# The product of maximum and scale in the softmax: from VectorE, behind the maximum, to ScalarE, ahead of the exponentials

## The chip, the cores and the metric

The kernel runs on one core of a Trainium2 chip. The metric is the device time of one execution in microseconds. Three runs of the kernel before took 1253.99, 1259.27 and 1259.77 us, median 1259.27 us.

## The reference

Two layers work on x, 2 batches of 2048 tokens of width 512 in float32. With ctx a context of 128 tokens per batch, and each branch scaled by the tanh of a gate:

```python
x = x + tanh(g_xattn[0]) * L0_xattn(layernorm(x), ctx)     # rotary cross attention, 8 heads of 64, softmax over 128
x = x + tanh(g_ffn[0])   * L0_ffn(layernorm(x))            # ternary weights, low-rank part, relu squared, 512 -> 2048 -> 512
x = x + tanh(g_xattn[1]) * L1_xattn(layernorm(x), ctx)     # linear on x and on the mean of ctx
x = x + tanh(g_ffn[1])   * L1_ffn(layernorm(x))            # rmsnorm, 8-bit activations, ternary weights, gelu
```

The change touches the softmax of the first attention: `attn = softmax(scores, axis=-1)` with `scores = einsum('bthd,bshd->bhts', q, k)`.

## The kernel before, in words

The 4096 tokens are worked in 16 groups g of 256 tokens, each of 2 tiles of 128. Every engine has one instruction stream that runs in order. ORDER holds, by hand, for each engine and each kind of step the places at which the step of each group stands in that stream; steps of neighbouring groups are interleaved, so that the attention of one group lies beside the first feed-forward layer and the second layer of the groups before it. At the start of the streams stand the preparation of the weights (ternary forms, transposes, scales) and the keys and values. The change alters no entry of ORDER.

A group has 4 softmax batches n, each of one tile of 128 tokens and 4 heads, so 64 batches over the kernel; they are called by group and batch below. A batch goes through these steps:

1. `scores` (TensorE, line 1659) writes 128x512 scores into one of three PSUM banks; from the fourth batch on it waits for the exponentials three batches earlier (s_exp), which frees the bank.
2. `soft_max` (VectorE): line 1373 reduces the bank to the negated maximum of each head, nmx (128x4), line 1377 multiplies it by sig, one number per partition, into nmb (128x4). Semaphores s_max and s_bias.
3. `exps` (ScalarE, line 937): waits for s_bias, then four activations Exp of 128x128 out of the bank with bias nmb and scale sig, each with its sum, and s_exp.
4. `soft_inv` (VectorE, line 1381) takes the reciprocal of the sums, `norm` (GpSimd, line 749) multiplies, `prob_hi` (ScalarE, line 948) and `prob_lo` (VectorE, line 1347) split the result into two float16 parts.
5. `turn_p` (SP queue, line 595) transposes both by DMA, and `p_v` (TensorE, line 1673) multiplies them with the values; its result goes through `pv_hi`, `pv_lo` and `out_proj` (line 1685) to `x1_out` (VectorE, line 1400).

Beside this, ScalarE's stream holds the relu and the two squares of the first feed-forward layer (`up_act`: lines 975, 980, 986) and its relu frees the banks of TensorE's line 1718; the Gelu, squares and conversion of the second (lines 996, 1002, 1007), and the high parts of transposed inputs (lines 926, 961, 992). Exp and Gelu are in different function tables: in the trace a load of tables (ACT_TABLE_LOAD) is found 13 times in front of an exponential and 14 times in front of a Gelu. GpSimd makes the low parts (line 744 for the hidden layer, line 723), the inverse roots (line 719) and some additions.

`need(eng, s, per, g, k)` is a wait of engine eng until semaphore s has the count that step k of group g brings.

Of the kernel before, what the change touches and what calls it, by code (L numbers as in the profile page):

```python
# [19 lines left out]
ACT = mybir.ActivationFunctionType  # L20
ALU = mybir.AluOpType
# [28 lines left out]
def build(nc, x_d, ctxT_d, gx_d, gf_d, wqT_d, wkvT_d, woT_d, fb_d, wfc_d, wproj_d, uT_d, vT_d, gate_d,  # L50
          wxT_d, wcT_d, bx_d, w1T_d, b1_d, w2T_d, b2_d, rope_d, mask_d, kv_d, out_d):
    ctx = ExitStack()
    with ctx:
        def sb(name, shape, dt):
            return ctx.enter_context(nc.sbuf_tensor(name, shape, dt))
# [66 lines left out]
        nmx = sb("nmx", [P, 4, 4], F32)  # L122
        nmb = sb("nmb", [P, 4, 4], F32)
# [28 lines left out]
        sig = sb("sig", [P, 1], F32)  # L152
# [15 lines left out]
        def att_bank(n):  # L168
            return ps[:, ATT0 + n % 3, :]
# [72 lines left out]
        def need(eng, s, per, g, k):  # L242

            if g >= 0:
                eng.wait_ge(s, g * per + (k + 1))
# [33 lines left out]
        def last_in(place):  # L279
# [226 lines left out]
            ACT=dict(wq=(1,), k_hi=(6,), v_hi=(7, 8), tanh=(5,), wo=(10,), kv_save=(17,),  # L506
                     evac=(22, 25, 29, 33, 36, 38, 41, 44), rows=(3, 4, 9, 12, 14, 15, 16, 18), low=(37,), wx=(32,),
                     sums=(30, 35, 39, 42, 45, 46, 47, 49), lift=(51, 52, 56, 58, 62, 75, 76, 82)),
# [31 lines left out]
        def first(g):  # L540
            return g == 0
# [288 lines left out]
        def _(act):  # L830
# [101 lines left out]
            def exps(g, n):  # L932
                if first(g) and n == 0:
                    act.wait_ge(c_kap, 1)
                need(act, s_bias, 4, g, n)
                for a in range(4):
                    last = act.activation(e[:, n, a * S:(a + 1) * S], att_bank(2 + n)[:, a * S:(a + 1) * S], ACT.Exp,  # L937
                                          bias=nmb[:, n, a:a + 1], scale=sig[:, :], accum_out=esum[:, n, a:a + 1])
                last.then_inc(s_exp, 1)
# [69 lines left out]
            def run():  # L1009
                for p in moments("ACT"):  # L1010
                    for m, g in due("ACT", "up", p):
                        up_act(g, m)
                    for t, g in due("ACT", "x1_hi", p):
                        x1_hi(g, t)
                    for hg, g in due("ACT", "rot", p):
                        rot_hi(g, hg)
                    for n, g in due("ACT", "exp", p):
                        exps(g, n)
                    for n, g in due("ACT", "p_hi", p):
                        prob_hi(g, n)  # L1020
                    for v, g in due("ACT", "pv", p):
                        pv_hi(g, v)
                    for t, g in due("ACT", "x2_hi", p):
                        x2_hi(g, t)
                    for _, g in due("ACT", "low", p):
                        low_first(g)
                    for t, g in due("ACT", "x3_hi", p):
                        x3_hi(g, t)
                    for t, g in due("ACT", "gelu", p):
                        gelus(g, t)  # L1030
                    for t, g in due("ACT", "q5", p):
                        q5_int(g, t)
                    prepare(p)
# [5 lines left out]
        def _(dve):  # L1039
# [330 lines left out]
            def soft_max(g, n):  # L1370
                need(dve, s_ps, 4, g, n)
                scores = att_bank(2 + n).rearrange("p (h s) -> p h s", h=4)
                dve.tensor_reduce(nmx[:, n, :], scores, axis=AX.X, op=ALU.max, negate=True).then_inc(s_max, 1)
                if first(g) and n == 0:
                    dve.wait_ge(c_kap, 1)
                need(dve, s_max, 4, g, n)
                dve.tensor_scalar(nmb[:, n, :], nmx[:, n, :], sig[:, :], None, ALU.mult).then_inc(s_bias, 1)  # L1377

            def soft_inv(g, n):
                need(dve, s_exp, 4, g, n)  # L1380
# [118 lines left out]
            def run():  # L1499
                for p in moments("DVE"):  # L1500
# [6 lines left out]
                    for n, g in due("DVE", "max", p):  # L1507
                        soft_max(g, n)
# [349 lines left out]
```

## Time and profile before

| | |
|---|---|
| median of 3 runs | 1259.27 us (1253.99 to 1259.77) |
| the profiled execution | 1254.16 us, span 1252.1 us |
| TensorE busy | 1120.1 us, 89% of the span |
| VectorE busy | 975.9 us, 78% |
| ScalarE busy | 783.7 us, 63% |
| GpSimd busy | 577.6 us, 46% |
| granted TensorE clock, mean | 0.96 |

The profile comes from one execution with its own time, which stands beside its span. In the rows, PE is the TensorE matmul, PEld its weight load, DVE is VectorE, ACT is ScalarE, POOL is GpSimd, SP the queue of transfers. Numbers of lines are lines of the kernel. Busy shares are means over the whole span, in which the first 300 us hold the preparation and the last 70 us the end of the last groups.

### The profile page before, as it was taken

The numbers are of one execution on the slowest core, as the hardware profiler recorded it, in microseconds if no ns is written. First come the engines' busy times: TensorE is split into PE (matmuls) and PEld (weight loads), VectorE is DVE, ScalarE is ACT, GpSimd is POOL, SyncE is SP. The second block draws the span as 40 slices with busy tenths as digits, with TensorE's granted clock in tenths as the row PEclk, the third lists the DMA queues.
The fourth block names the chain that finished last, engine by engine and source line by source line (L and its number), as shares of the span: only waits on it lengthen the run. The fifth ranks groups of instructions, "written<-read, shape, count | busy, mean of one in ns | idle before, by whom it ended". The sixth has DMA issues, their size and how long they took to land.

```text
span 1252.1 us, 19955 instructions
## 1 busy us (share of the span) xinstructions
PE 1120.1 (89%) x7102; PEld 697.7 (56%) x7390; DVE 975.9 (78%) x2029; ACT 783.7 (63%) x1509; POOL 577.6 (46%) x564
## 2 busy tenths in 40 slices
PE   5737788989999999999899999999999999999973
PEld 3525546565665656474656565575657465565631
DVE  5998877678779787978877888878876867877672
ACT  2588765758393947576485858385767657585622
POOL 3121465445564644554545455555545443644330
PEclk9757799999999999999999999999999999999997
DMA  9959843463625354444536362637354353524122
GB/s 312 348 141 319 224 117 73 71 130 64 128 54 135 65 113 86 102 98 100 118 64 143 62 142 51 125 66 127 73 95 108 66 115 61 108 58 81 30 59 51
DMA packets 302242, 140.28 MB, mean 112 GB/s; under 512 B 258097, under 2 KB 276017, under 8 KB 300465
## 3 DMA queue, kind: packets, MB, share of 16 engines
q1 hardware_dynamic: 299840, 136.62, 48.7%
q10 hardware_dynamic: 2304, 2.40, 0.6%
q8 instruction: 57, 0.93, 0.3%
q14 instruction: 41, 0.33, 0.1%
HBM read 57.97 MB, written 9.18 MB: 54 GB/s over the span
## 4 chain that ended last, share of the span: by engine, by line
PE 30%; DVE 27%; ACT 20%; DMA 11%; issue 6%; POOL 4%; SPq 2%; POOLq 0%; ACTq 0%; DVEq 0%
PE ps L1734 8%; ACT e L937 5%; PE ps L1782 4%; PE ps L1685 4%; PE ps L1718 3%; ACT rl L975 3%; PE ps L1770 3%; DVE st L1334 3%; DMA pt<-qT 3%; PE ps L1750 3%; ACT hid L980 2%; DVE qT L1347 2%; ACT sq L986 2%; DVE amax L1041 2%; DMA hT<-q 2%
## 5 line engine op out<-in xcount | busy, mean ns | idle before, releaser
L1718 PE MATMUL ps<-xT,fcT 128*128 128x256 f16 x2048 | 261.4, 276 | 7.1 <-ACT rl L975 7.1
L719 POOL TENSOR_TENSOR rs<-ve,nhalf 128x1 f32<-128x1 f32 x160 | 105.3, 660 | 321.7 <-DVE ve L1339 226.4
L1734 PE MATMUL ps<-pjT,hid 128*128 128x512 fp8e4 x1024 | 232.6, 380 | 2.6 <-issue 1.3
L1718 PEld LDWEIGHTS ps<-xT,fcT 128*128 128x128 fp8e4 x2048 | 202.2, 99 | 42.2 <-ACT rl L975 10.2
L744 POOL TENSOR_TENSOR hid<-sq,hid 128x512 f16<-128x512 f32 x128 | 155.9, 1221 | 114.0 <-ACT sq L986 113.6
L1734 PEld LDWEIGHTS ps<-pjT,hid 128*128 128x128 f16 x1024 | 97.7, 98 | 98.9 <-issue 1.3
L1782 PE MATMUL ps<-w2T,hT 128*128 128x512 fp8e4 x512 | 119.9, 389 | 23.0 <-DMA hT<-q 22.8
L975 ACT ACTIVATE rl<-ps,rsf 128x256 f32<-128x256 f32 x256 | 106.5, 469 | 43.5 <-PE ps L1722 43.5
L1770 PE MATMUL ps<-w1T,q4T 128*128 128x512 fp8e4 x512 | 122.9, 383 | 5.6 <-DMA q4T<-x16b 4.5
L1007 ACT ACTIVATE q<-h 128x2048 f16<-128x2048 f32 x32 | 61.1, 1909 | 104.4 <-DVE h L1491 104.4
L937 ACT ACTIVATE e<-ps,nmb,sig 128x128 f32<-128x128 f32 x256 | 113.1, 458 | 4.7 <-DVE nmb L1377 4.5
L1347 DVE TENSOR_TENSOR qT<-e,qT 128x512 f16<-128x512 f32 x96 | 88.9, 935 | 25.0 <-ACT qT L948 16.1
L1480 DVE SCALAR_TENSOR_TENSOR h<-ps,dqs,b1bc 128x512 f32<-128x512 f32 x128 | 91.7, 741 | 14.6 <-PE ps L1770 13.1
L749 POOL TENSOR_TENSOR e<-e,einv 128x512 f32<-128x512 f32 x64 | 68.9, 1081 | 67.9 <-DVE einv L1381 67.8
L1750 PE MATMUL ps<-wx,xT 128*128 128x512 f16 x384 | 89.5, 383 | 10.7 <-DMA xT<-x16b 10.6
L1041 DVE TENSOR_REDUCE amax<-h 128x1 f32<-128x2048 f32 x32 | 73.0, 2281 | 31.6 <-ACT h L996 31.6
L1639 PE MATMUL ps<-pt,wq 128*128 128x256 f16 x768 | 89.2, 276 | 8.1 <-issue 6.6
L1639 PEld LDWEIGHTS ps<-pt,wq 128*128 128x128 f16 x768 | 75.6, 99 | 22.6 <-issue 12.3
L1685 PE MATMUL ps<-wo,qS 128*128 128x512 f16 x384 | 85.5, 379 | 0.0
L980 ACT ACTIVATE hid<-rl 128x512 f16<-128x512 f32 x128 | 80.6, 630 | 5.0
L1782 PEld LDWEIGHTS ps<-w2T,hT 128*128 128x128 f16 x512 | 50.2, 100 | 57.3 <-issue 5.5
L986 ACT ACTIVATE sq<-rl 128x512 f32<-128x512 f32 x128 | 78.5, 613 | 0.0
(207 smaller groups left out, 1998.8 us busy)
## 6 DMA issues: line engine op xcount, KB each, us to landing
xb<-in_x SPq DMA_DIRECT2D x16, 512.0 KB, 4.2
qS<-qT SPq DMA_DIRECT2D x128, 64.0 KB, 2.1
out<-r SPq DMA_DIRECT2D x32, 256.0 KB, 2.4
xa<-in_x SPq DMA_DIRECT2D x15, 512.0 KB, 4.4
rope<-in_rope SPq DMA_DIRECT2D x16, 384.0 KB, 3.4
h<-in_w1T SPq DMA_DIRECT2D x6, 1024.0 KB, 6.2
h<-in_w2T SPq DMA_DIRECT2D x6, 1024.0 KB, 6.4
h<-in_wkvT SPq DMA_DIRECT2D x2, 1024.0 KB, 16.1
```

The costliest lines, as they stand in the source:

```text
L744: pool.tensor_tensor(flat[:, 1, :], sq[:, m % 2, :], flat[:, 0, :], ALU.subtract).then_inc(hid_lo, 1)
L937: last = act.activation(e[:, n, a * S:(a + 1) * S], att_bank(2 + n)[:, a * S:(a + 1) * S], ACT.Exp, bias=nmb[:, n, a:a + 1], scale=sig[:, ...
L975: act.activation(rl[:, m % 2, a * G:(a + 1) * G], ps[:, FFN0 + m % 2, a * G:(a + 1) * G], ACT.Relu, scale=rsf[:, 2 * m + a:2 * m + a + 1]) ...
L980: act.activation(hid[:, 0, 2 * m:2 * m + 2, :].rearrange("p c n -> p (c n)"), rl[:, m % 2, :], ACT.Square)\
L1347: dve.tensor_tensor(dst, src, hi, ALU.subtract).then_inc(done, 1)
L1639: mm = pe.matmul(att_bank(hg)[:, a * G:(a + 1) * G], wq[:, ws, k, c:c + P], xT1[:, xs, k, :], start=(n == 0 and k == 0), stop=(n == 2 and ...
L1685: mm = pe.matmul(att_bank(8 + t), ao[:, xs, k, t * P:(t + 1) * P], wo[:, ws, k, :], start=(n == 0 and k == 0), stop=(n == 2 and k == KC - 1))
L1718: pe.matmul(dst, fcT[:, k, f * P:(f + 1) * P], xT2[:, xs, k, :], start=(xs == 0 and k == 0), stop=False)
L1734: mm = pe.matmul(ps[:, FFN0 + t, :], hid[:, xs, c, t * P:(t + 1) * P], pjT[:, c, :], start=(c == 0 and xs == 0), stop=(c == FC - 1 and xs ...
L1750: mm = pe.matmul(back_bank(t), xT3[:, xs, k, t * P:(t + 1) * P], wx[:, ws, k, :], start=(n == 0 and k == 0), stop=(n == 2 and k == KC - 1))
L1770: mm = pe.matmul(back_bank(2 + u), q4T[:, k, t * P:(t + 1) * P], w1T[:, k, n * 512:(n + 1) * 512], start=(k == 0), stop=(k == KC - 1))
L1782: mm = pe.matmul(back_bank(10 + t), hT[:, t, c, :], w2T[:, c, :], start=(c == 0), stop=(c == FC - 1))
```

## The change

ScalarE makes nmb itself, just ahead of the four exponentials of the batch. It waits for the maximum (s_max) in the place where it waited for s_bias, issues one activation Copy of 128x4 from nmx to nmb with scale sig, and then waits for its own result by s_bias. VectorE's line 1377 goes, with its waits for s_max and, once, for c_kap. The number of instructions in total stays the same. Places in the streams, tiles and the values' formula stay.

```diff
             def exps(g, n):
                 if first(g) and n == 0:
                     act.wait_ge(c_kap, 1)
+                need(act, s_max, 4, g, n)
+                act.activation(nmb[:, n, :], nmx[:, n, :], ACT.Copy, scale=sig[:, :]).then_inc(s_bias, 1)
                 need(act, s_bias, 4, g, n)
                 for a in range(4):
                     last = act.activation(e[:, n, a * S:(a + 1) * S], att_bank(2 + n)[:, a * S:(a + 1) * S], ACT.Exp,
@@
             def soft_max(g, n):
                 need(dve, s_ps, 4, g, n)
                 scores = att_bank(2 + n).rearrange("p (h s) -> p h s", h=4)
                 dve.tensor_reduce(nmx[:, n, :], scores, axis=AX.X, op=ALU.max, negate=True).then_inc(s_max, 1)
-                if first(g) and n == 0:
-                    dve.wait_ge(c_kap, 1)
-                need(dve, s_max, 4, g, n)
-                dve.tensor_scalar(nmb[:, n, :], nmx[:, n, :], sig[:, :], None, ALU.mult).then_inc(s_bias, 1)
```

## Rows read from the trace of the kernel before

**Rows 1.** The page: busy us, share of the span, instructions of each engine.

```profile
PE 1120.1 (89%) x7102; PEld 697.7 (56%) x7390; DVE 975.9 (78%) x2029; ACT 783.7 (63%) x1509; POOL 577.6 (46%) x564
```

**Rows 2.** Windows: busy us by engine; columns PE, PEld, DVE, ACT, POOL, clock, DMA, GB/s.

```profile
300.00:1180.00 880.00, 846.90 (x5494) 526.67 (x5730) 701.36 (x1478) 569.86 (x1119) 443.76 (x432) 1.00 0.46 92
```

**Rows 3.** The page: the chain that ended last, by engine and by line.

```profile
PE 30%; DVE 27%; ACT 20%; DMA 11%; issue 6%; POOL 4%; SPq 2%; POOLq 0%; ACTq 0%; DVEq 0%
PE ps L1734 8%; ACT e L937 5%; PE ps L1782 4%; PE ps L1685 4%; PE ps L1718 3%; ACT rl L975 3%; PE ps L1770 3%; DVE st L1334 3%; DMA pt<-qT 3%; PE ps L1750 3%; ACT hid L980 2%; DVE qT L1347 2%; ACT sq L986 2%; DVE amax L1041 2%; DMA hT<-q 2%
```

**Rows 4.** Groups of VectorE by line and shape: busy us, mean ns, idle before.

```profile
L1377 DVE TENSOR_SCALAR nmb<-nmx,sig 128x4 f32<-128x4 f32 x64 | 31.1, 486 | 2.3
```

**Rows 5.** Instructions on the tile nmx: durations in ns, shortest, median, longest.

```profile
L1373 DVE TENSOR_REDUCE nmx<-ps x64: 651/680/693, 72.2 to 1105.2; 128x4 f32<-128x512 f32 x64
L1377 DVE TENSOR_SCALAR nmb<-nmx,sig x64: 229/327/1192, 72.9 to 1105.9; 128x4 f32<-128x4 f32 x64
```

**Rows 6.** Timeline of VectorE at 416 us: start, us, engine, line, operation.

```profile
416.45 1.19 DVE L1377 TENSOR_SCALAR nmb<-nmx,sig 128x4 f32<-128x4 f32 x1
```

**Rows 7.** Timeline of GpSimd at the same moment.

```profile
416.45 1.15 POOL L744 TENSOR_TENSOR hid<-sq,hid 128x512 f16<-128x512 f32 x1 [0.66 <-ACT sq L986]
```

**Rows 8.** The chain in order of time (start, us, what): first and last of twelve.

```profile
490.08 0.07 DVE nmb L1377
...
1040.48 0.04 DVE nmb L1377
```

**Rows 9.** Timeline of VectorE at 824 us.

```profile
824.16 1.14 DVE L1377 TENSOR_SCALAR nmb<-nmx,sig 128x4 f32<-128x4 f32 x1
825.21 0.54 DVE L1343 TENSOR_SCALAR xa<-xa,mv,rs 128x512 f32<-128x512 f32 x1
```

**Rows 10.** Waits of ScalarE: who for whom, us, times, longest.

```profile
ACT e L937 <- DVE nmb L1377: 4.5, 5, 1.5
```

**Rows 11.** Groups of ScalarE by line and shape.

```profile
L937 ACT ACTIVATE e<-ps,nmb,sig 128x128 f32<-128x128 f32 x256 | 113.1, 458 | 4.7 <-DVE nmb L1377 4.5
...
L1007 ACT ACTIVATE q<-h 128x2048 f16<-128x2048 f32 x32 | 61.1, 1909 | 104.4 <-DVE h L1491 104.4
...
L843 ACT ACTIVATE wq<-hid,winv 128x2048 f16<-128x2048 f32 x1 | 2.0, 2004 | 0.0
...
L888 ACT ACTIVATE tg<-graw 128x4 f32<-128x4 f32 x1 | 0.2, 187 | 0.0
```

**Rows 12.** Timeline of ScalarE from 616 to 622 us.

```profile
616.59 0.62 ACT L986 ACTIVATE sq<-rl 128x512 f32<-128x512 f32 x1
617.22 1.28 ACT L937 ACT_TABLE_LOAD   x1
618.52 0.46 ACT L937 ACTIVATE e<-ps,nmb,sig 128x128 f32<-128x128 f32 x1
...
620.28 0.84 ACT L975 ACTIVATE rl<-ps,rsf 128x256 f32<-128x256 f32 x2
621.15 0.63 ACT L980 ACTIVATE hid<-rl 128x512 f16<-128x512 f32 x1
621.69 0.61 ACT L986 ACTIVATE sq<-rl 128x512 f32<-128x512 f32 x1
```

**Rows 13.** The chain in order of time: first and last piece entered in ScalarE's order.

```profile
77.87 1.38 ACT e L937 x7
...
962.56 3.51 ACT e L937 x16
```

**Rows 14.** Timeline of ScalarE at 1096 us.

```profile
1096.39 1.28 ACT L937 ACT_TABLE_LOAD   x1
1098.68 0.46 ACT L937 ACTIVATE e<-ps,nmb,sig 128x128 f32<-128x128 f32 x1 [1.01 <-DVE nmb L1377]
```

**Rows 15.** Timeline of VectorE at 1097 us.

```profile
1097.69 0.69 DVE L1373 TENSOR_REDUCE nmx<-ps 128x4 f32<-128x512 f32 x1 [0.39 <-PE ps L1659]
```

## The prediction

> **What bounds the kernel now.** I read the busy shares first: TensorE is at 89%, VectorE at 78%, ScalarE at 63% [rows 1]. The windows view shows where the 89% comes from: from 300 to 1180 us TensorE is busy for 846.90 of 880 us at a granted clock of 1.00, so it idles for 33 us there; the rest of its idle time is in the preparation and in the tail, where no softmax is left [rows 2]. That looks like a kernel that no vector work can move. The chain of waits says otherwise: of its length TensorE has 30%, VectorE 27% and ScalarE 20%, and the exponentials of line 937 alone have 5% [rows 3]. The two agree if the small holes in TensorE's stream come at the end of long chains over ScalarE and VectorE: an earlier result closes a hole of a fraction of a microsecond at most, a later one widens it by its full length. Earlier is worth less than later costs. That asymmetry decides this case more than the price of an instruction.
>
> **What goes from VectorE.** Line 1377 runs 64 times, 31.1 us in all, mean 486 ns [rows 4]. Its duration is of two kinds. At its shortest it takes 229 ns, at its longest 1192 [rows 5]. At 416.45 us VectorE's small product and a GpSimd subtraction start together, and the product ends at 417.64 us, just behind the GpSimd instruction (416.45 + 1.15 = 417.60) [rows 6, 7]. It was held for the length of that instruction, while the maximum from PSUM before it is never held (651 to 693 ns over all 64) [rows 5]. So of 31.1 us some 16 us (64 x (486 - 229 ns)) is waiting for GpSimd. The Trainium skill has a rule for this (SBUF — State Buffer, "There are two physically separate sides"): VectorE in a two-port mode and GpSimd take an exclusive lock on one pair of ports for the whole instruction. The trace agrees. By the rule a hold taken from VectorE may be met again by the next such instruction, and by it up to 16 us of holds could go; by the rows of the chain only the part below does.
>
> What lies on the chain: I went through the chain over the whole span and found the product in it 14 times. Twelve of these are passed in VectorE's order, the first at 490.08 and the last at 1040.48 us [rows 8]. Without the product the next instruction could start some 0.60 us behind the maximum's start (0.69 us less the overlap of 0.09 that unlinked neighbours have, see below). Its actual start less that gives 0.25, 0.55, 1.00, 0.34, 1.17, 0.25, 0.35, 1.17, 0.25, 0.34, 0.42 and 0.40 us. The fifth, at 824.16 us, is a hold whose next instruction, a product of SBUF data on line 1343, would be held by the same GpSimd instruction, so I strike it [rows 9]. The eleven others make 5.3 us. The thirteenth is at the very first softmax (72.9 us), where ScalarE waits for the product: its exponentials start at 74.17 us, maximum done at 72.84; with my price below they would start at about 73.2, a gain of 1.0 us. The fourteenth, at 752.76 us, comes out even. Gain on the chain: **6.3 us** (7.5 if the fifth counts). ScalarE waits for the product only 5 times, 4.5 us [rows 10]; in the other 59 batches it arrives later than the product, so the shorter latency of the maximum to the bias gains nothing.
>
> **What comes to ScalarE.** 64 activations Copy of 128x4 with the scale from a tile. No such row exists. The nearest is the tanh of 128x4 without such a scale: 187 ns. What a scale out of a tile adds is seen at 128x2048: 2004 ns for line 843 with one against 1909 ns for line 1007 without, 95 ns [rows 11]. So 187 + 95 = 0.28 us, bounds 0.19 (the scale hidden) and 0.46 (a whole 128x128 exponential from PSUM, 458 ns). I take 0.28, the bound below being much the nearer in size. Next, the exponential must wait for the Copy's own semaphore. Unlinked neighbours overlap: the square of line 980 at 621.15 us ends at 621.78, and the one of line 986 starts at 621.69. Linked ones do not: the two relu end at 621.12 and the square that reads them starts at 621.15 [rows 12]. So the Copy takes the exponentials' old start, 0.09 before the end of the previous instruction, and they start 0.28 + 0.03 behind it: each batch is late by **0.31 us**.
>
> The chain passes 33 batches of exponentials in ScalarE's order, first at 77.9 us, last the piece up to 966.07 us; these two are shown [rows 13]. In 26 of them no table load stands ahead: 26 x 0.31 = 8.1 us. In six a table load stands ahead, which already started without overlap; there the Copy slips partly into that gap and costs 0.18: 1.1 us. In the seventh (group 8, 617.22 us) the Copy must moreover wait for the maximum, which ends at 617.27: the load would start at 617.60 in place of 617.22, 0.4 us [rows 12]. Sum on the chain: **9.6 us**, and by the bounds of the Copy 7 to 15 us. Off the chain the other copies are covered: ScalarE is 570 of 880 us busy in the steady part [rows 2].
>
> **The table load.** One thing that is now free: at 1096.39 us the load of 1.28 us runs while ScalarE waits for the product; the exponential then starts at 1098.68 [rows 14]. The load stands in front of the first Exp; a Copy stands in front of that, and waits for the maximum, which ends at 1098.38 [rows 15]. Load and wait then follow each other: 1098.41 + 0.28 + 0.02 + 1.28 = 1099.99 and the exponentials at about 1100.0, 1.3 us later. The same count gives 1.3 at 1032.36, 0.5 at 888.26 and 0.5 at 746.54 us: 3.6 us in four groups. None of the four is on the chain, and how much slack they have no row says. I count 0.5 us of it, and all 3.6 is the bound. The page ScalarE: Activation LUTs of the Trainium skill ("What ACT_TABLE_LOAD costs") adds a drain of about 1.4 us to each load. By it a switch costs twice as much; the trace shows none, since at 617.22 the load starts 0.01 us behind the square and the exponential 0.02 us behind the load's end [rows 12], so the sum has no such term.
>
> **The sum.** At first order, +9.6 - 6.3 = +3.3 us. As a cost on the chain is paid in full and a gain only as far as the next path behind allows (which itself has become 0.3 us per batch longer), I let half to all of the 6.3 us count: +3.3 to +6.5 us, plus 0.5 for the loads, **+5 us**. The profiled execution took 1254.16 us (span 1252.1), so 1259.2 by its own measure. The three runs shown have 1253.99, 1259.27 and 1259.77 us: two levels 5 us apart, with the profile on the lower one and the median on the upper. I do not know on which the new kernel's median falls, and take half that offset: **1262 us**. What a measurement of this kernel can tell from no change is about 0.5%, 6.3 us.
>
> **The rivals.**
> A, the copies and loads bite in full: ScalarE's in-order path becomes the one that sets the softmax everywhere, the gains of VectorE are all covered by it, and the four loads come onto the path. +9.6 + 3.6 = +13 us; with a Copy of 0.45 us +19. For it: 33 of 64 batches on the chain are ScalarE's, and only 12 VectorE's. Against: in groups 10 to 12 and 14 the chain is VectorE's. 1267 by the profile's measure. It decides where a batch's Copy starts at the end of the preceding ScalarE instruction rather than at the end of the maximum.
> B, TensorE hides all: its 33 us of idle time are spread over other causes (transfers, the tail of a group), and both sides vanish. 0 us, 1254 to 1259. For it: 96% busy. Against: the chain crosses the softmax in nearly each group.
> C, the other sign: VectorE's freed 31 us count, ScalarE's added 18 us (64 x 0.28) do not, having 310 us of idle time in the steady part to hide in. -6.3 on the chain, -7.5 with the fifth hold: about 1247. It would need the copies to run while ScalarE waits anyway, which it does in only 5 of 64 batches; that is what speaks against it.
>
> **How the numbers follow.** Forecast (+3 to +7) 0.35, A 0.30, B 0.15, C 0.20. A is slower by over 0.5%, and a quarter of the forecast reaches over it: 0.39. Within 0.5% lie the rest of the forecast and B: 0.41. C is faster: 0.20. Range: from C (1247 and, with half the offset of the median, 1249) to A with the same offset (1254.2 + 13.2 + 2.6 = 1270) and a little of its larger Copy: 1249 to 1271. The likeliest case's own range is 1257 to 1266.
>
> **What would show it.** Line 1377 gone from VectorE, and its busy time down by about 31 us, if the holds by GpSimd do not pass to lines 1343, 1469, 1471 and 1491, whose means would then rise; a new ScalarE row of 64 at about 0.28 us (0.19 would lower the cost on the chain to 7); exponentials starting 0.03 us behind the Copy; the thirteen loads standing behind a Copy, and at some 1100 us an exponential 1.3 us later against its maximum. The number of ScalarE's waits for the maximum should be near 5. The forecast is wrong if the chain after loses ScalarE's share or TensorE's idle time between 300 and 1180 us falls below 33 us: then C. It is also wrong if the load starts while the maximum is still running, for then it would stand ahead of the Copy.

## The result, and the profile after

The changed kernel takes 1265.29 us at the median of 7 runs (1263.84 to 1267.95); the kernel before, with its later runs on the same chip, 1255.54 us (7 runs, 1251.91 to 1259.77). The ratio is 1.0088, 95% interval 1.0064 to 1.0112: 11 us slower, 8 to 14 by the interval. The time lies in the predicted range, and its sign is that of the forecast; the forecast of +5 us was about half of what came. The upper level on which the first median of before stood (1259.27) was no property of the kernel: over 7 runs it is 1255.54.

The page of the profiled execution (1263.84 us, span 1261.8): busy us by engine, and the chain that ended last, by engine and by line.

```profile
PE 1120.1 (89%) x7102; PEld 694.1 (55%) x7390; DVE 951.7 (75%) x1965; ACT 801.3 (64%) x1573; POOL 576.3 (46%) x564
...
PE 29%; ACT 27%; DVE 21%; DMA 11%; issue 5%; POOL 4%; SPq 2%; POOLq 0%; DVEq 0%; ACTq 0%
PE ps L1732 8%; ACT e L939 8%; ACT rl L977 4%; PE ps L1780 4%; PE ps L1683 4%; PE ps L1716 4%; ACT hid L982 3%; PE ps L1768 3%; ACT sq L988 3%; DMA hT<-q 3%; DMA pt<-qT 2%; DVE st L1336 2%; PE ps L1748 2%; ACT qT L950 2%; DVE qT L1349 2%
```

VectorE is busy for 24.2 us less than in [rows 1], ScalarE for 17.6 more, TensorE for exactly as long. In the chain of waits (the path that ended last) ScalarE has gone from 20% to 27% and VectorE from 27% to 21% [rows 3]; the exponentials alone from 5% to 8%.

The windows view of 300 to 1180 us, for [rows 2]:

```profile
300.00:1180.00 880.00, 842.12 (x5471) 520.73 (x5706) 678.13 (x1424) 579.79 (x1163) 441.61 (x431) 1.00 0.45 92
```

TensorE's idle time there is 38 us in place of 33, and since its work comes later, less of it fits into the stretch. The instructions on the tile nmb (durations in ns: shortest, median, longest):

```profile
L936 ACT ACTIVATE nmb<-nmx,sig x64: 280/283/317, 72.6 to 1119.9; 128x4 f32<-128x4 f32 x64
```

The timeline of ScalarE at the first batch of group 5 and of group 15:

```profile
416.86 0.61 ACT L988 ACTIVATE sq<-rl 128x512 f32<-128x512 f32 x1
417.38 0.28 ACT L936 ACTIVATE nmb<-nmx,sig 128x4 f32<-128x4 f32 x1
417.69 1.28 ACT L939 ACT_TABLE_LOAD   x1
418.98 0.46 ACT L939 ACTIVATE e<-ps,nmb,sig 128x128 f32<-128x128 f32 x1
...
1108.02 0.30 ACT L936 ACTIVATE nmb<-nmx,sig 128x4 f32<-128x4 f32 x1 [2.06 <-DVE nmx L1375]
1108.34 1.28 ACT L939 ACT_TABLE_LOAD   x1
1109.63 0.46 ACT L939 ACTIVATE e<-ps,nmb,sig 128x128 f32<-128x128 f32 x1
```

The Copy takes 283 ns as priced, starts 0.09 us before the square ends, and the load stands behind it. At 1108 us the load that ran during the wait [rows 14] now follows it. ScalarE waits for the maximum 5 times (4.7 us), as often as was predicted.

Where VectorE's freed time went is told by its waits (waited for, us in total, times, longest). Before:

```profile
DVE einv L1381 <- ACT e L937: 43.2, 25, 3.9
```

After:

```profile
DVE einv L1379 <- ACT e L939: 69.7, 37, 4.5
DVE qT L1349 <- ACT qT L950: 21.2, 25, 2.4
```

The reciprocal, which needs the exponentials' sums, waits 26.5 us longer for ScalarE. This growth has two sources of about equal size, as two of the runs below show: with the product gone and no Copy the wait is 55.6 us (run 1), with a Copy and the product kept it is 55.8 (run 2). VectorE comes earlier and the exponentials come later, and at the reciprocal the one waits for the other. Who waits for ScalarE on TensorE, before and after:

```profile
PE ps L1718 <- ACT rl L975: 7.1, 5, 3.9
PE ps L1734 <- ACT rl L975: 1.0, 2, 0.6
```

```profile
PE ps L1716 <- ACT rl L977: 11.3, 10, 4.3
PE ps L1732 <- ACT rl L977: 4.5, 5, 1.1
```

The relu of the feed-forward layer stands in ScalarE's stream behind the exponentials and is late with them; it frees the bank that TensorE needs next. These two waits of TensorE grow by 7.7 us together.

The two timelines laid side by side give the shift of each batch's first exponential. In ScalarE's runs of batches it grows by 0.31 to 0.35 us from one batch to the next, as in group 5 (after less before): +6.38, +6.70, +7.05, +7.37. By group, shift of the first batch in us:

```
group  0    1    2    3    4    5    6    7    8    9    10   11   12   13   14    15
us   -1.3 -1.1 +0.1 +3.7 +5.8 +6.4 +6.0 +6.4 +7.4 +8.1 +9.7 +9.3 +9.7 +9.4 +11.5 +11.0
```

The gain of the first softmax is there (-1.3, 1.0 predicted), used up by group 2. The steep part, from group 2 to 4, has more than copies in it: see the clock below. This is one pair of traces, and one execution differs from the next by some microseconds.

### The profile page after: what moved, and what is told of

The parts are those of the page before. It is cut to its first block, busy times and chain, and to the rows that moved or that the text cites. A ratio compares the mean times of both kernels' runs of the same rounds, so it can differ in the third digit from the quotient of the medians.

```text
span 1261.8 us, 19954 instructions
## 1 busy us (share of the span) xinstructions
PE 1120.1 (89%) x7102; PEld 694.1 (55%) x7390; DVE 951.7 (75%) x1965; ACT 801.3 (64%) x1573; POOL 576.3 (46%) x564
## 4 chain that ended last, share of the span: by engine, by line
PE 29%; ACT 27%; DVE 21%; DMA 11%; issue 5%; POOL 4%; SPq 2%; POOLq 0%; DVEq 0%; ACTq 0%
PE ps L1732 8%; ACT e L939 8%; ACT rl L977 4%; PE ps L1780 4%; PE ps L1683 4%; PE ps L1716 4%; ACT hid L982 3%; PE ps L1768 3%; ACT sq L988 3%; DMA hT<-q 3%; DMA pt<-qT 2%; DVE st L1336 2%; PE ps L1748 2%; ACT qT L950 2%; DVE qT L1349 2%
## 5 line engine op out<-in xcount | busy, mean ns | idle before, releaser
L1716 PE MATMUL ps<-xT,fcT 128*128 128x256 f16 x2048 | 258.3, 274 | 11.5 <-ACT rl L977 11.3
L1349 DVE TENSOR_TENSOR qT<-e,qT 128x512 f16<-128x512 f32 x96 | 91.8, 965 | 30.1 <-ACT qT L950 21.2
L1043 DVE TENSOR_REDUCE amax<-h 128x1 f32<-128x2048 f32 x32 | 73.0, 2281 | 31.1 <-ACT h L998 31.0
```

What stands on the lines that cost most here:

```text
L1349: dve.tensor_tensor(dst, src, hi, ALU.subtract).then_inc(done, 1)
L1716: pe.matmul(dst, fcT[:, k, f * P:(f + 1) * P], xT2[:, xs, k, :], start=(xs == 0 and k == 0), stop=False)
```

## The experiments

Ratios are to the kernel before, run on the same chip, with their 95% intervals; in microseconds they are taken times 1254. Their edits are against the kernel named.

**1. The product gone, no Copy.** Against the changed kernel:

```diff
+                if first(g) and n == 0:
+                    act.wait_ge(c_const, 4)
                 need(act, s_max, 4, g, n)
-                act.activation(nmb[:, n, :], nmx[:, n, :], ACT.Copy, scale=sig[:, :]).then_inc(s_bias, 1)
-                need(act, s_bias, 4, g, n)
...
-                                          bias=nmb[:, n, a:a + 1], scale=sig[:, :], accum_out=esum[:, n, a:a + 1])
+                                          bias=nhalf[:, :], scale=sig[:, :], accum_out=esum[:, n, a:a + 1])
```

> The product of maximum and scale is left out altogether: none on VectorE, no Copy on ScalarE; the exponentials wait for the maximum and take a constant column as their bias, so this leaves the subtraction of the maximum out. It is the change without its cost. Theory 1 (the gains of VectorE are covered, since the exponentials already start at the end of the preceding ScalarE instruction and not at the end of the product): 0 to 3 us under the kernel before, ratio 0.998 to 1.000. Theory 2 (the gain of 6.3 us on the chain is real and the measured +0.88% comes from a cost far over 9.6 us): 6 to 8 us under it, ratio about 0.994 to 0.995.

Measured: 0.995 (0.9931 to 0.9969), -6.3 us (-8.7 to -3.9). That is Theory 2's value: the gain is not covered by ScalarE, and its size is that of the chain, 6.3 us. In its trace the shift of the attention's end (the line 1400 of before) is -1.7 us in group 2, -2.2 in group 9 and -5.2 in group 13. The exponentials start 1.3 us earlier from the first softmax on (1.0 was counted), gain 0.8 us from group 6 to 7 (0.8 counted) and 2.9 us in groups 10 to 12 (3.4 counted); the 1.2 us counted in group 14 are not seen in their starts. So the gain falls in the main where the chain passed the product.

**2. The Copy added, the product kept.** Against the kernel before; nmj is a new tile, and the count of c_tanh, which ScalarE itself raises once before, serves as the link:

```diff
                 need(act, s_bias, 4, g, n)
+                act.activation(nmj[:, n, :], nmx[:, n, :], ACT.Copy, scale=sig[:, :]).then_inc(c_tanh, 1)
+                act.wait_ge(c_tanh, 4 * g + n + 2)
```

> The kernel before, with its product on VectorE, and one more Copy of 128x4 with a scale from a tile on ScalarE ahead of each batch's exponentials, linked to them by a semaphore; its result is read by nobody. It is the change without its gain. Theory 1: the 9.6 us of the on-path copies in full, plus little for the table loads: 9 to 13 us over before, ratio 1.008 to 1.010. Theory 2: 15 us or more over before, ratio 1.012 or more, so that less 6.3 us it gives the measured 1.0088. Rival (TensorE covers copies): under 1.004.

Measured: 1.0154 (1.0133 to 1.0175), +19.3 us (16.7 to 21.9). Theory 1 of that run falls: the cost is twice the 9.6 us. Together with run 1, -6.3 + 19.3 = +13.0 us, the whole change of +11.0 (8 to 14) within the intervals. Within these intervals the change is the sum of its two parts, and the error of the forecast is in the larger. If each of the 64 batches were late by its 0.31 us in full, it would be 19.8 us. Its chain:

```profile
PE 28%; ACT 27%; DVE 23%; DMA 10%; issue 6%; POOL 4%; SPq 2%; POOLq 0%; ACTq 0%; DVEq 0%
```

**3. A second Copy, not linked.** Against the changed kernel:

```diff
+                act.activation(nmj[:, n, :], nmx[:, n, :], ACT.Copy, scale=sig[:, :])
                 act.activation(nmb[:, n, :], nmx[:, n, :], ACT.Copy, scale=sig[:, :]).then_inc(s_bias, 1)
```

> The changed kernel with a second Copy of 128x4 ahead of the first, not linked to anything, result read by nobody. Slope of the time against ScalarE's in-order path. Theory 1: each of the 64 copies adds 0.28 less the overlap of 0.09 = 0.19 us; with 33 to all 64 batches on the path +6 to +12 us over the changed kernel, ratio to before 1.014 to 1.018. Rival (the 0.9% came from something else, such as the clock or the transfers): ratio stays near 1.009.

Measured: 1.0227 (1.0202 to 1.0251), 17 us over the changed kernel (13 to 22), above both expectations. In its timeline the two copies start 0.19 us apart (360.24 and 360.43), so 64 of them are 12.2 us. The rest may in part be the clock: the mean granted clock of its five runs leaves 54.2 us of lost clock (span times one less the clock), that of the changed kernel's seven 47.6 us. With the 0.4 us of time for each microsecond of lost clock at the end of this document, an estimate, that is 2.6 us. It is not shown.

**4. The table load ahead of the wait.** Against the changed kernel:

```diff
+                if n == 0:
+                    if first(g):
+                        act.wait_ge(c_const, 4)
+                    act.activation(nmj[:, :], nhalf[:, :], ACT.Exp)
                 need(act, s_max, 4, g, n)
```

> The changed kernel with a small Exp of one column ahead of the wait for the maximum in the first batch of each group, so that the table load runs while ScalarE waits, as before. Theory 1 (the four delayed loads are off the path): it costs the small Exp, 0.19 us in 16 groups, 0 to +3 us on the changed kernel, ratio to before 1.009 to 1.011. Rival A of the prediction (the delayed loads of 3.6 us are paid): 2 to 3.6 us under the changed kernel, ratio 1.006 to 1.007.

Measured: 1.0101 (1.0081 to 1.0121), 1.6 us over the changed kernel, not under it; the two intervals together leave -2.3 to +5.5. In its trace the load runs ahead of the maximum again (at 1106.08 us, right behind the square). But the run also adds 16 small exponentials of 0.20 us, 3.2 us of ScalarE's time, and a gain from the loads can be hidden by their cost. So this run alone does not show what the late loads are worth; run 9 limits it.

**5 and 6. The Copy of run 2 on the chain only, and off it only.** Against the kernel before; nmj is the tile of run 2, and ON_PATH holds the 33 batches (numbered 4g + n) that the chain of before passes in ScalarE's order:

```diff
+            ON_PATH = (1, 2, 5, 6, 7, 8, 9, 10, 11, 12, 13, 14, 16, 17, 18, 20, 21, 22, 24, 32, 33, 34, 35, 36, 37, 38, 39, 42, 46, 47, 52, 53, 54)
...
+                if 4 * g + n in ON_PATH:
+                    act.activation(nmj[:, n, :], nmx[:, n, :], ACT.Copy, scale=sig[:, :]).then_inc(c_tanh, 1)
+                    act.wait_ge(c_tanh, sum(1 for u in range(4 * g + n + 1) if u in ON_PATH) + 1)
```

> The kernel before with the extra Copy only in the 33 batches that its chain of waits passes in ScalarE's order (of groups 0 to 6, 8 to 11 and 13). All 64 of them cost 1.54%, 19 us, twice the 9.6 us that were counted. Theory 1 (the price per batch is right and the batches off the chain cost too, since their slack is under 0.3 us or used up): 9 to 12 us, ratio 1.007 to 1.010. Theory 2 (the price of a batch on the chain is 0.6 us and not 0.31, those off it are free): 17 to 20 us, ratio 1.014 to 1.016.

Measured: 1.0103 (1.0084 to 1.0123), +12.9 us (10.5 to 15.4).

> The same with the Copy only in the 31 other batches, those that the chain of the kernel before does not pass in ScalarE's order, the four delayed table loads among them. Theory 1: 7 to 10 us, ratio 1.006 to 1.008, so that with the 33 others it makes the 19 us. Theory 2: 0 to 2 us, ratio 1.000 to 1.002.

This run has the same edit with `not in ON_PATH` in both places. Measured: 1.0042 (1.0026 to 1.0057), +5.3 us (3.3 to 7.1). The sum is 18.2 us, within run 2's interval. The main part of the error is here: 31 copies that were priced at nothing, but for 0.5 us for the late loads among them, cost 5.3 us, 0.17 each. The page of run 6 shows how:

```profile
PE 31%; ACT 25%; DVE 23%; DMA 10%; issue 5%; POOL 4%; SPq 2%; DVEq 0%; ACTq 0%
```

With copies in only those batches the chain has moved to ScalarE, 25% in place of 20%. The exponentials have 62.6 us of the chain before, 58.9 in run 1, 96.4 in run 6, 102.3 after the change and 98.2 in run 2; at 1.9 us a batch that is 33, 31, 51, 54 and 52 batches. The chain of before names one longest path; since copies of 0.3 us off it cost time, some of the next ones must have been less than 0.3 us behind. The second trace of the unchanged kernel (run 11) says the same: counted by the batches of which most lies in the chain, both traces have 35, but only 31 of them are the same ones.

**7 and 8. No product, and the scale a constant.** A version that needs no product: the preparation multiplies the query weights by the constant 1/8 and the keys by 1, so that sig is 1 and the negated maximum is the bias. Against the changed kernel, whose Copy and wait for s_bias go as well; the last pair of lines is that of run 8.

```diff
-                    dve.reciprocal(kvinv[:, :], kvmaxa[:, :]).then_inc(c_kvinv, 1)
+                    dve.memset(kvinv[:, 0:1], 1.0)
+                    dve.reciprocal(kvinv[:, 1:2], kvmaxa[:, 1:2]).then_inc(c_kvinv, 1)
...
-                    dve.tensor_scalar(sig[:, :], wmaxa[:, 0:1], kvmaxa[:, 0:1], HD ** -0.5, ALU.mult, ALU.mult)\
-                        .then_inc(c_kap, 1)
+                    dve.memset(sig[:, :], 1.0).then_inc(c_kap, 1)
...
-                dve.reciprocal(winv[:, a:b], wmaxa[:, a:b]).then_inc(c_wscale, 1)
+                if a == 0:
+                    dve.memset(winv[:, a:b], HD ** -0.5).then_inc(c_wscale, 1)
+                else:
+                    dve.reciprocal(winv[:, a:b], wmaxa[:, a:b]).then_inc(c_wscale, 1)
...
-                                          bias=nmb[:, n, a:a + 1], scale=sig[:, :], accum_out=esum[:, n, a:a + 1])
+                                          bias=nmx[:, n, a:a + 1], scale=1.0, accum_out=esum[:, n, a:a + 1])
```

In run 7 the scale is still read from sig, which holds 1.

> A version without any product: query weights scaled by 1/8 and keys by 1 in the preparation, where they were scaled to a maximum of 64, so that sig is 1 and the negated maximum itself is the bias; scale still read from a tile that holds 1. Its steady part is that of the kernel with the product left out. Theory: as that one, ratio 0.993 to 0.997.

Measured: 0.9936 (0.992 to 0.9952), -8.0 us; as run 1.

> The version without a product, and the exponentials' scale a constant of the instruction. By the 95 ns that a scale from a tile cost at 128x2048, each of 256 exponentials gets 0.09 us shorter, 0.36 us a batch. If a batch is worth its length nearly everywhere, as the added copies showed, -0.36 x 64 = -23 us on the version before this one; as a gain is cut off by the next path, half to three quarters of it: ratio to before 0.978 to 0.986. If gains are cut off at once, under 5 us: 0.991 or more.

Measured: 0.9888 (0.987 to 0.9906), -14.0 us (-16.3 to -11.8), median 1239.76 us. It beats both kernels. The groups of ScalarE in run 7 and in run 8:

```profile
L937 ACT ACTIVATE e<-ps,nmx,sig 128x128 f32<-128x128 f32 x256 | 113.0, 458 | 1.7 <-DVE nmx L1376 1.4
```

```profile
L937 ACT ACTIVATE e<-ps,nmx 128x128 f32<-128x128 f32 x256 | 89.9, 371 | 2.5 <-DVE nmx L1376 2.3
```

An exponential is 87 ns shorter without the scale from a tile, but of 22 us only 6 us (3 to 9 by the two intervals) became time: about a quarter, where half to three quarters were expected. The chain of run 8 fits that: TensorE has 45% of it, ScalarE 11%.

```profile
PE 45%; DVE 23%; ACT 11%; DMA 9%; issue 5%; POOL 4%; SPq 2%; POOLq 0%; DVEq 0%; ACTq 0%
```

**9 and 10. The off-chain copies, divided.** As run 6, with the list (40, 48, 56, 60), the four batches with a delayed load, and with the 27 others.

> The kernel before with the extra Copy only in the four batches whose table load ran during the wait for the product (first batches of groups 10, 12, 14 and 15); they were charged with 3.6 us and are off the chain. Theory 1 (the 5 us of the off-chain copies are the delayed loads): 3 to 5 us, ratio 1.0025 to 1.004. Theory 2 (the loads have slack): 0 to 1 us, ratio 0.999 to 1.001.

Measured: 1.001 (0.9988 to 1.0031), +1.3 us (-1.5 to +3.9). In its timeline the load is late as counted (1098.86 us, behind the Copy). The value fits Theory 2 best, but the interval holds the lower part of Theory 1, the 3.6 us of the prediction's bound included.

> The same with the Copy in the 27 remaining batches, off the chain and without a delayed load. Theory 1: 0 to 2 us, ratio 1.000 to 1.0015. Theory 2 (small slack is used up, the chain moves to ScalarE in groups 7, 10, 12, 14, 15): 4 to 6 us, ratio 1.003 to 1.005.

Measured: 1.0024 (1.0005 to 1.0044), +3.0 us (0.6 to 5.5), between the two theories. Runs 9 and 10 together are 4.3 us, within run 6's interval. The division among them is not settled; that plain batches off the chain cost something is.

**11 and 12. Second traces of the kernel before and of the changed one, unchanged.**

> The kernel before once more, unchanged, for a second trace: where TensorE's granted clock falls between 200 and 1180 us. If the stretches at the lower clock belong to the program they come at the same places (430 and 1140 us); if they differ from execution to execution, they come elsewhere or in another number, and account for part of the spread of its times of about 8 us.

> The changed kernel once more, unchanged, for a second trace. If the fall of the clock at 265 and 290 us belongs to the change it is there again; if not, the steps of 2 and 1 us that the first trace has there are chance, and the shift in group 4 is about 3 us smaller.

Windows of the first trace of before and of the changed kernel (the third figure from the right is the granted clock):

```profile
265.00:275.00 10.00, 9.17 (x69) 6.72 (x71) 7.06 (x15) 4.67 (x10) 4.44 (x4) 1.00 0.60 135
...
440.00:450.00 10.00, 10.00 (x52) 4.43 (x53) 6.56 (x12) 3.62 (x4) 1.97 (x4) 0.88 0.14 26
```

```profile
265.00:275.00 10.00, 7.38 (x37) 4.02 (x39) 7.71 (x16) 1.95 (x4) 4.76 (x4) 0.83 0.57 132
285.00:295.00 10.00, 7.34 (x37) 4.12 (x39) 8.00 (x21) 9.87 (x31) 6.34 (x7) 0.83 0.14 26
```

and of the second trace of before:

```profile
260.00:270.00 10.00, 7.50 (x39) 3.88 (x38) 9.31 (x20) 2.27 (x4) 6.70 (x6) 0.83 0.76 125
...
880.00:890.00 10.00, 7.65 (x47) 5.20 (x46) 5.93 (x15) 5.40 (x13) 1.61 (x2) 0.83 0.52 131
```

A row of 10 us with a granted clock of 0.83 had a third of its time at 1.2 GHz and the rest at 2.4. In the first trace of before, that is found twice, about 430 to 450 and 1140 to 1160 us; in the second (1258.84 us, against 1254.16) at these places and also at 260 and 880 us. The step at 880 puts that execution 1.8 us behind the first within one group. In both traces of the changed kernel (the second at 1261.46 us) the clock falls at about 265 and between 280 and 300 us, and not at 430 and 1140. Ahead of 265 us TensorE had stood waiting for the transfer into hT in all four traces: for 3.14 and 2.75 us in those of the changed kernel, for 2.50 us in the second of before, and for 2.49 us in the first, where the clock did not fall. So part of the places belongs to the program and part to chance. In the shift between the first pair of traces, read on VectorE's instructions, these stretches are steps: +2.0 at 265 us and about +1.2 at 290 us against the changed kernel, -1.3 at 440 and -1.7 at 1150 us in its favour. They nearly cancel, and so do not explain the 11 us. Nor does the mean lost clock, 47.6 us over the changed kernel's seven runs and 48.6 to 50.9 for the kernel before in its three sets of runs. The second pair of traces has the shift of group 15 at +6.8 us in place of +11.0, and is 2.6 us apart in time: the size of the effect is read from the many runs, not from a pair of traces.

## Why the prediction was right in sign and range, and short by half

- **The asymmetry, earlier is worth less than later costs: wrong for the gain it was applied to.** VectorE's 6.3 us on the chain came in full: -6.3 in run 1, -8.0 in run 7. To let only half to all of it count was a guess, and no row stood behind it. That it raised the forecast from +3.8 to +5 us, nearer to the measured 11, was luck. The asymmetry is there only further on: of run 8's next 22 us a quarter counted.
- **Which instructions were the gain: right in the main.** The first softmax and the places in groups 6 and 10 to 12 are where the shift of run 1 falls; those in group 14 are not seen in it. Run 1 tested the removal as a whole; what of it was arithmetic and what holds by GpSimd was not divided. VectorE's busy time fell by 24.2 us and not 31.1, since holds were met by the next instructions, as the rival reading had it: the low parts of the probabilities and queries (lines 1347 before, 1349 after) went from 88.9 to 91.8 us, the layer norm's line 1343 (1345) on xa from 21.4 to 22.5, and the conversion of line 1471 (1469) from 22.7 to 23.8.
- **The price of a batch: right.** 283 ns measured for 0.28, 0.31 to 0.35 us from batch to batch. The 95 ns for the scale came from the longest of three such instructions of line 843 (2004 ns); the two others take 1987 and 1985, which would have given 0.26 to 0.27.
- **"Off the chain the other copies are covered": the step that failed.** That ScalarE idles for 310 us says nothing about whether it idles just where a Copy is put in. 31 such copies cost 5.3 us (3.3 to 7.1).
- **The copies on the chain: 9.6 us predicted, 12.9 measured (10.5 to 15.4).** The term was too small by 3.3 us, or just by 0.9 at the interval's end. The clock does not make up for it: the mean lost clock is 52.3 us over run 5's six runs and 50.9 over the twelve of before beside them, by the slope below 0.6 us. Where the rest comes from stays open.
- **The table loads: right in place and time (1.3 us late against the maximum in groups 14 and 15); the charge of 0.5 us is not contradicted.** Run 9 gives +1.3 us (-1.5 to +3.9) for the same four batches, which leaves room for 0.5 and, barely, for all 3.6. Run 4 does not decide it, since its small exponentials cost time as well.
- **Rival A** had the right mechanism in half: ScalarE's in-order path became the one that sets the softmax in most groups (about 54 batches in the chain for 33), and its number for it, +13 us, is nearer to the measured +11 than the forecast's +5. But it had VectorE's gains covered, which run 1 refutes, and the loads paid in full, which no run shows; the copies off the chain stand in their place. **B** and **C** fall: run 2 shows no cover by TensorE, and 19 us for 18 us of added ScalarE work. Of C, the gain of 6.3 us was real.
- In all: 12.9 + 5.3 - 6.3 = +11.9 us for the measured 11.0. The forecast's +5 was 9.6 + 0 + 0.5 less the discounted gain. Its 1262 us for the median holds a further 2.6 us for a level on which the kernel before does not stand over more runs (1255.54); so the time came within 3.3 us of the forecast where the difference was off by 6.

## What to carry to other kernels

A chain of waits names one longest path, and for an added cost the sum over it was too low here: the next paths were in part closer than the cost itself. 0.31 us put on all 64 batches cost 19 us, as if all 64 stood on the path, where the 33 of the chain had been counted. A removed cost, on the contrary, was worth what the chain gave for it as long as it was small (6 of 1254 us), and about a quarter once TensorE had most of the chain. Before moving a small product between engines, ask whether a scale chosen in the preparation makes it unnecessary: that gave 0.6%, and 1.1% with the constant it allows.

## What the runs showed of the hardware that was not expected

- A product of 128x4 on VectorE, 229 ns at its shortest, took 16.4 us more than 64 times that, and up to 1192 ns for one, in a kernel whose GpSimd is busy for 46%. In the trace of before 38 of the 64 are longer than 260 ns, and each of these ends 0.02 to 0.04 us behind the end of a GpSimd instruction, while the maximum on the same engine, which reads PSUM, stays at 651 to 693 ns.
- A scale read from a tile costs ScalarE about the same at 4 columns (283 for 187 ns, a Copy against a tanh), at 128 (458 for 371) and at 2048 (1985 to 2004 for 1909), 76 to 96 ns: in an instruction of 128 columns that is a fifth.
- The spread of the kernel's times goes in part with TensorE's clock: over 46 runs of the kernel before, the time and the lost clock (span times one less the mean granted clock) have a correlation of 0.47, and 0.40 us of time for each microsecond of it. Over the seven runs of the changed kernel (42.9 to 53.2 us lost) it is 0.95 and 0.38, but over the six of run 5 there is none (-0.13); which of the two causes the other is not shown.
